# Splitting exponentials between VectorE and GpSimd, three to five, in the first two batches of an attention and mixture-of-experts kernel, with the router sums moved behind the hidden low part

## The reference

```python
attn = jnp.einsum('bhqd,bhkd->bhqk', q, k) * scale
attn = jax.nn.softmax(attn, axis=-1)
out = jnp.einsum('bhqk,bhkd->bhqd', attn, v)
...
g = jnp.einsum('bsh,ehf->ebsf', x, w_gate)
u = jnp.einsum('bsh,ehf->ebsf', x, w_up)
h = jax.nn.silu(g) * u
expert_out = jnp.einsum('ebsf,efh->ebsh', h, w_down)
cw = router_probs * gate_weights
cw = cw / (jnp.sum(cw, axis=-1, keepdims=True) + 1e-09)
out = jnp.einsum('ebsh,bse->bsh', expert_out, cw)
```

## Time and profile before

| | |
|---|---|
| median of three runs | 2798.79 us (2797.85 to 2798.8) |
| profiled execution | 2797.0 us, span 2794.7 us |
| TensorE clock granted, mean | 0.993 |
| busy | PE 2726.0 us (98%), DVE 2173.4 (78%), POOL 1737.4 (62%), ACT 1694.6 (61%) |
| chain that ended last | PE 88%, DVE 6%, ACT 2% |

### The profile page before, as it was taken

How to read it: one execution, slowest core, us unless ns; L and a number is a source line. 1 busy time by engine, 2 the same in 40 slices (tenths; PEclk the granted TensorE clock), 3 DMA queues, 4 the chain that set the end, 5 groups by cost and what they waited for, 6 DMA issues and landing times.

```text
span 2794.7 us, 47289 instructions
## 1 busy us (share of the span) xinstructions
PE 2726.0 (98%) x16416; PEld 2236.9 (80%) x16416; DVE 2173.4 (78%) x3254; ACT 1694.6 (61%) x3240; POOL 1737.4 (62%) x1630
## 2 busy tenths in 40 slices
PE   7789999999999999999999999999999999999998
PEld 5578878888888888878888788888888888888887
DVE  7977788777877787787787888778878778776665
ACT  7756566665666666666665666656666665544443
POOL 5656666666666566666665666765666666655554
PEclk9999999999999999999999999999999999999999
DMA  2113233232323323323232322323223233333332
GB/s 69 39 57 98 77 95 95 89 104 79 95 93 91 103 76 96 95 88 102 80 92 90 99 91 87 95 83 110 90 77 99 76 102 91 95 106 112 107 104 81
DMA packets 251273, 252.25 MB, mean 90 GB/s; under 512 B 15904, under 2 KB 242848, under 8 KB 251040
## 3 DMA queue, kind: packets, MB, share of 16 engines
q1 hardware_dynamic: 251040, 249.25, 29.3%
HBM read 240.66 MB, written 8.52 MB: 89 GB/s over the span
## 4 chain that ended last, share of the span: by engine, by line
PE 88%; DVE 6%; issue 3%; ACT 2%; POOL 0%; DMA 0%; SPq 0%; POOLq 0%; ACTq 0%; DVEq 0%
PE ps_o L692 23%; PE ps_s L658 23%; PE ps_t L658 23%; PE ps_s L751 4%; PE ps_t L761 3%; PE ps_m L547 3%; PE ps_a L733 2%; PE ps_a L735 2%; DVE h_lo L946 1%; PE ps_m L595 1%; PE ps_m L555 1%; PE ps_m L602 1%; DVE hf L941 1%; PE ps_m L610 1%; DVE hf L934 1%
## 5 line engine op out<-in xcount | busy, mean ns | idle before, releaser
L946 DVE TENSOR_TENSOR h_lo<-hf,h_hi 128x512 fp32r<-128x512 f32 x512 | 493.5, 964 | 229.6 <-ACT h_hi L780 221.7
L780 ACT ACTIVATE h_hi<-hf 128x512 fp32r<-128x512 f32 x512 | 323.9, 633 | 466.3 <-DVE hf L941 466.2
L934 DVE SCALAR_TENSOR_TENSOR hf<-hf,ps_s 128x512 f32<-128x512 f32 x512 | 350.4, 684 | 298.7 <-ACT hf L775 293.5
L775 ACT ACTIVATE hf<-ps_s 128x512 f32<-128x512 f32 x512 | 305.5, 597 | 350.8 <-PE ps_s L658 212.7
L1168 POOL TENSOR_TENSOR wg_lo<-stage_w,wg_hi 128x512 fp32r<-128x512 f32 x256 | 339.8, 1327 | 235.5 <-ACT wg_hi L787 235.3
L692 PE MATMUL ps_o<-h_hi,wd_hi 128*128 128x512 f32 x1024 | 401.4, 392 | 18.9 <-DVE h_lo L946 18.9
L1228 POOL TENSOR_TENSOR Pt_lo<-Pt 128x512 f16<-128x512 f32 x256 | 295.0, 1152 | 186.5 <-ACT Pt L913 185.5
L692 PE MATMUL ps_o<-h_lo,wd_hi 128*128 128x512 f32 x1024 | 399.4, 390 | 0.0
L692 PE MATMUL ps_o<-h_hi,wd_lo 128*128 128x512 f32 x1024 | 398.6, 389 | 0.0
L1168 POOL TENSOR_TENSOR wd_lo<-stage_w,wd_hi 128x512 fp32r<-128x512 f32 x256 | 338.1, 1321 | 91.9 <-ACT wd_hi L787 91.9
L941 DVE TENSOR_TENSOR hf<-hf,ps_t 128x512 f32<-128x512 f32 x512 | 351.9, 687 | 38.1 <-PE ps_t L658 0.7
(11 more groups left out here) (190 smaller groups left out, 5135.8 us busy)
## 6 DMA issues: line engine op xcount, KB each, us to landing
stage_w<-in_L_ffn_w_gate_dram SPq DMA_DIRECT2D x256, 256.0 KB, 2.7
stage_w<-in_L_ffn_w_up_dram SPq DMA_DIRECT2D x256, 256.0 KB, 2.9
stage_w<-in_L_ffn_w_down_dram SPq DMA_DIRECT2D x256, 256.0 KB, 2.7
cwb<-d_cw SPq DMA_DIRECT2D x64, 256.0 KB, 3.7
X<-in_x_dram SPq DMA_DIRECT2D x32, 256.0 KB, 3.1
C<-in_fside_BxSxS_dram SPq DMA_DIRECT2D x16, 256.0 KB, 3.0
KVM<-in_ctx_dram SPq DMA_DIRECT2D x16, 256.0 KB, 2.7
d_x<-X SPq DMA_DIRECT2D x16, 256.0 KB, 2.1
```

The costliest lines, as they stand in the source:

```text
L775: act.activation(hf[:], ps_g[:], ACT.Tanh, scale=0.5).then_inc(tanh_done, 1)
L780: act.activation(h_hi[f % FC][:], hf[:], ACT.Copy).then_inc(hh_done, 1)
L934: dve.scalar_tensor_tensor(out=hf[:], in0=hf[:], scalar=1.0, in1=ps_g[:], op0=ALU.add, op1=ALU.mult).then_inc(gate_done, 1)
L946: dve.tensor_tensor(h_lo[f % FC][:], hf[:], h_hi[f % FC][:].bitcast(F32), ALU.subtract).then_inc(hl_done, 1)
```

## The change

Two things change. In batches 0 and 1, which end before the joint stage begins, VectorE takes the items 1, 4 and 6 of each eight (three), and GpSimd the items 0, 2, 3, 5 and 7 (five). From batch 2 on the split is as before. Since the counts per batch now differ, TensorE's waits take their values from a running sum. And in every turn, VectorE's router instructions stand behind h_lo and the weighted outputs of the step instead of ahead of the attention sums.

```diff
@@ -55,6 +55,7 @@
     DVE_LOW = (1, 3, 5, 7)
+    DVE_LOW_ALONE = (1, 4, 6)
@@ -392,12 +393,15 @@
-        def by_dve(i):
-            return i % OCT in DVE_LOW
-
-        def low_parts(i, dve):
-
-            return sum(by_dve(j) == dve for j in range(i))
+        def by_dve(b, i):
+            alone = (b + 1) * STEPS <= START
+            return i % OCT in (DVE_LOW_ALONE if alone else DVE_LOW)
+
+        low_parts = {True: [0], False: [0]}
+        for b in range(B):
+            for i in range(STEPS):
+                for dve in (True, False):
+                    low_parts[dve].append(low_parts[dve][-1] + (by_dve(b, i) == dve))
@@ -719,8 +723,8 @@
                         if i == first:
-                            turn.wait(pe, lo_dve, d, low_parts(i + 4, True))
-                            turn.wait(pe, lo_pool, d, low_parts(i + 4, False))
+                            pe.wait_ge(lo_dve, low_parts[True][(turn.b + d) * STEPS + i + 4])
+                            pe.wait_ge(lo_pool, low_parts[False][(turn.b + d) * STEPS + i + 4])
@@ -1036,8 +1040,6 @@
-                    router_weights(turn, step)
-
                     d, i = item_at(step, 1 - BEHIND)
@@ -1066,12 +1068,13 @@
                         low_of(f + 1)
                     if f is not None and f % EXPERT == EXPERT - 1:
                         weigh_output(f, 1)
+                    router_weights(turn, step)
```

More of the change, by code:

```diff
@@ L225, in bass_xattn_moe_ffn_kernel @@
         t_ps = Count("t_ps", 32); exp_done = Count("exp_done", 32)
-        lo_dve = Count("lo_dve", STEPS // OCT * len(DVE_LOW)); lo_pool = Count("lo_pool", STEPS - lo_dve.per)
+        lo_dve = sem("lo_dve"); lo_pool = sem("lo_pool")
         av_ps = Count("av_ps", 32)
@@ L1068, in body @@
                         weigh_output(f, 1)
+                    router_weights(turn, step)
                     d, i = item_at(step, -1)
-                    if turn.has(d) and by_dve(i):
+                    if turn.has(d) and by_dve(turn.b + d, i):
                         turn.wait(dve, exp_done, d, i + 1)
@@ L1073, in body @@
                         dve.tensor_tensor(Pt_lo[slot][:], Pt[slot][:], Pt[slot][:].bitcast(BF16)[:, 1::2],
-                                          ALU.subtract).then_inc(lo_dve.sem, 1)
+                                          ALU.subtract).then_inc(lo_dve, 1)
                     name, k, d, one, _ = misc(turn, step)
@@ L1224, in body @@
                     d, i = item_at(step, -1)
-                    if turn.has(d) and not by_dve(i):
+                    if turn.has(d) and not by_dve(turn.b + d, i):
                         turn.wait(pool, exp_done, d, i + 1)
@@ L1228, in body @@
                         pool.tensor_tensor(Pt_lo[slot][:], Pt[slot][:], Pt[slot][:].bitcast(BF16)[:, 1::2],
-                                           ALU.subtract).then_inc(lo_pool.sem, 1)
+                                           ALU.subtract).then_inc(lo_pool, 1)
                     for o, at, d in v_at(turn):
```

## The result

The changed kernel takes **2806.7 us** (median of 8 runs, 2804.3 to 2808.16), the kernel before 2798.14 us beside it (8 runs): ratio 1.0031, 95% interval 1.0022 to 1.004. It is slower by 8.6 us; 13 were forecast. The profiled execution took 2804.47 us, its span 2802.5 us against 2794.7, so 7.8 us longer.

The account below looks back on a forecast made before the run. TensorE, busy 98%, bounds the kernel, so only its waits count. Profiled execution 2797.0 + 10 (early stage) + 3 (joint stage) = 2810.0 us; the median lies 1.8 above, 2811.8, said as 2812; range 2796 to 2826.

Parts of the forecast that it names:

- Early stage, +10 forecast: Batches 0 and 1: delayed groups cost 11.7 us, VectorE's relief takes 1.7 off; bounds -5.6 and +19.
- what the last low part loses, each four loses: Early stage: a loop in which TensorE's products with the values wait for the low part of each four's last item.
- relief: Early stage: VectorE's 5.6 us less work shortens TensorE's waits for maxima by a quarter, 1.7 us.
- The fourth row: Early stage, items 47, 51, 55: item 47 has slack for all, 0; items 51 and 55 -0.4 and +0.5 us.
- The split is neutral: Rival, early stage: VectorE's lighter load brings maxima and mq early enough, early 0, joint +3, 2802 us; chance 0.17.
- relief wins: Rival, early stage: half of VectorE's waits go (-3.9 us) and no group is late, 2798 us; chance 0.08.
- Joint stage, +3 forecast: Joint stage: twelve turns each 0.2 us longer, 2.4 us, and 0.3 in each of two turns; bounds -17.6, +15.6.
- The replay of the second step: Joint stage: h_lo done at 357.0 instead of 357.95, TensorE waits 0.4 us; gate product at 360.25 instead of 359.75.
- The gain of 1.0 is given back: Joint stage: TensorE starts 1.0 us earlier after h_lo, then loses that and 0.2 us more per turn.
- The first half of the replay: Joint stage: h_lo, at 349.31, wins against acc's second half, ends at 350.0 instead of 352.17; the 0.92 us wait goes.
- The turn is lost: Rival, joint stage: acc's second half beats h_lo, gate product 1.2 us later, +1.3 us a turn, 2824 us; chance 0.13.
- The router waits really go: Rival, joint stage: moved sums fall into GpSimd's gaps, all 17.6 us of h_lo waits gained, 2791 us; chance 0.12.

Follow-up runs that it names:

- Experiment 3: Kernel before, router unmoved; in batches 0 and 1 VectorE takes items 1, 3, 7 of each eight, GpSimd five: 2796.8 us, ratio 0.9994.
- experiment 4: Kernel before, router unmoved; in batches 0 and 1 VectorE takes items 0, 2, 4, 6 and GpSimd 1, 3, 5, 7: 2813.43 us, ratio 1.0056.
- experiment 2: Kernel before with only the router moved behind h_lo, split 1, 3, 5, 7 kept: 2794.53 us, ratio 0.9992.
- experiment 7: Kernel before, router unmoved, but from batch 2 on item 19's low part goes to GpSimd: 2801.23 us, ratio 1.0013.
- experiment 1: Kernel before with only the split 1, 4, 6 for VectorE in batches 0 and 1, router unmoved: 2806.41 us, ratio 1.0033.
- Experiment 9: Kernel before with the router moved and cprod, css, cden, cw made one-input reciprocals (output numbers differ): 2777.01 us, ratio 0.9928.
- experiment 6: Kernel before with the router moved and, from batch 2 on, item 19's low part on GpSimd; early split unchanged: 2794.79 us, ratio 0.999.

## Why the prediction was right, and where it wasn't

**Early stage, +10 forecast, +8.2 measured.** The step "what the last low part loses, each four loses" held: in 15 of 16 groups TensorE's products start 0.10 to 0.15 us after GpSimd's low part, and experiments 3 and 4 show that it is the item. The two prices held as well: from the exponential's end to the low part's end item 27 takes 0.75 us more than before (forecast 0.8, taken as 0.75) and item 23 1.15 (1.15, taken as 1.2). How much later than before each four's products started, as an increment over the four ahead:

```
items            forecast        measured
3 11 19 27 43 59 6 x 0.75 = 4.5  .92 .76 .66 .53 -.49 1.18 = 3.6
15 23 31 63      4 x 1.2 = 4.8   .52 1.95 1.28 1.29        = 5.0
7 35 39          2.3             .72 1.85 1.04             = 3.6
47 51 55         0.1             -1.54 -.89 .07            = -2.4
behind item 63                   -1.6
relief           -1.7            not separate
sum              10.0            8.2
```

The sizes of the even and odd groups are right within 1 us together; single groups are not. One trace is a weak witness for a single group: in experiment 2, whose code is that of before up to step 51, item 23 is 1.3 us late and items 43 and 47 get 2.5 us back, and in experiment 7 neither happens.

The fourth row failed. The forecast gave item 47 nothing, since it had slack; but its 1.7 us of slack took up delay of the groups ahead, here 1.54 us, and the same 1.54 in experiment 1. This has nothing to do with the router, which comes later. Of items 51, 55 and 59 the router's move took 1.4 us off (experiment 1 has increments of -.57, .72 and 1.60 there), and by the first gate that is gone again. I had priced the move at nothing outside the joint stage; in the change that came out, by luck, since with the splits 1, 3, 5, 7 and 1, 3, 7 the same move gains 3.0 to 3.5 us in the same stretch (experiment 2).

The relief was put at a quarter of the waits for maxima, 1.7 us. No run measures it: in the change it is contained in the increments, and the -1.6 us behind item 63 only look like it (in experiment 1 they are -3.0). So the sum of 8.2 against 10 is in part luck: delays of 12.2 us in the first three rows, against 11.6 forecast, and 4.0 us of recovery, against 1.6, for which the forecast had another reason.

**The split is neutral, relief wins.** Both fell: their 2802 and 2798 us, ratios of 1.0014 and 1.000, lie below the intervals of the change and of experiment 1. (The 3 us in them are the forecast's joint stage, which did not come; without them they lie lower still.) Experiment 3 shows the condition under which they hold, with the last items kept.

**Joint stage, +3 forecast, -0.4 measured.** The replay of the second step came out on the trace (after minus 8.2 us): ATT until 355.2 (forecast 355.1), h_lo done at 356.9 (357.0), cden held until 357.8 (358.0), negmax done at 359.4 (359.6), the gate product at 360.0 (360.25); TensorE's wait for h_lo is 0.38 us (0.4), and the wait for a maximum is new in each of twelve turns. "The gain of 1.0 is given back" is what the three distances show: -0.94, then +0.99. Only the 0.2 us a turn beyond it were too much: it was 0.05 in this turn and 0.2 us in all twelve together, where 2.4 were forecast, and the 0.6 us for two further turns did not come. The first half of the replay was right in its result and wrong on the way: h_lo did not win the race against acc and end at 350.0, but lost it and ended at 351.2 (after minus 8.2 us). TensorE wanted it at 351.3, so the first wait still went, with 0.1 us to spare; that is luck.

**The turn is lost** happened as an event and not as a price. h_lo came at 357.51, as forecast, and acc's second half, at 357.54, went ahead. But the price of 1.3 us a turn was wrong: I let cprod and css each wait for one of GpSimd's instructions. Only cprod waited (0.91); css followed in the same gap (0.15). The gate product then stood at 361.03, where it stood before, shifted. The forecast for the first step, with its win, and this loss meet at the same instruction of GpSimd, the low part ending at 360.29.

**The router waits really go** was refuted for this change and confirmed as a mechanism. It was said to decide from a saving of about 1.0 us of such waiting a turn, and to bring all 17.6 us then. Experiment 9 removes the waiting of the four and brings 17.8 us in the twelve turns. In the change the waiting of css and cw (1.31 and 1.03 us) did go, to 0.15 and 0.17; but cprod, cden, ATT and the first h_lo took it over, with 0.91, 0.99, 1.04 and 1.87 us. Taking each instruction's shortest time off, the router's four, ATT and the two h_lo of the turn shown waited 4.4 us in all before and 4.6 us in the change (an estimate from VectorE's timelines). The rival did not ask who waits in their place.

The rule of the Trainium skill, "SBUF — State Buffer", section "SBUF: two separate sides", that the loser of the port blocks for the whole instruction, agrees with every such line, down to two elements (cden, 0.99 us). The same section of the Trainium skill limits it to VectorE instructions with two SBUF inputs or in a two-port mode; experiment 9 agrees, as its one-input reciprocals took 0.12 to 0.25 us in the same places. The sentence of the Trainium skill, "Perfetto Trace Analysis", section "Optimizing Scalar/DVE Operations", that moving work between the two might not help, is borne out by experiment 6, with nothing gained (joint 2623.8 against 2623.9).

## What to carry to other kernels

Before work is dealt out to two engines, ask which item of each group is waited for, and leave that one on the engine that reaches it first; the count mattered less here (3 to 5 with the right items is free, and 4 to 4 with the wrong ones costs 16 us). Moving short instructions out of the way of a long wait gives back what it gains when they still stand ahead of the next thing that is waited for; measure distances between the starts of one repeated product, step by step, since a list of waits drops the small ones. Where VectorE and GpSimd keep each other waiting, as here, the thing to schedule is the port's time: look for the stretch in which VectorE's short two-input instructions stand, and move GpSimd's work out of it, as the exchange of two items did for 5.8 us.

## What the hardware showed that I had not expected

- Of VectorE's instructions only some wait for GpSimd. In the changed kernel maxima (negmax, 0.63 to 0.69 us in all 512), reciprocals (rsum, 0.19 to 0.20) and the gate product, which has one operand in PSUM (0.67 to 0.69 us in all 512), took the same time whether GpSimd was at work or not. Two of these, negmax and rsum, read PSUM; but the sums lsum and csum, which read SBUF, stayed at 0.12 to 0.18 us as well. Those with two SBUF inputs took up to 1.88 us for 0.68. But so did TENSOR_SCALAR with one tensor in SBUF: 0.40 to 0.41 us in the eight that started beside no instruction of GpSimd, 1.20 us (median, at most 1.39) in the 56 that started inside one.
- The race turns on hundredths. h_lo, dispatched 0.03 us before the start of GpSimd's next half of acc, lost and took 1.87 us; in the twelve turns it was dispatched from 0.04 us before to 0.01 us after that start, and lost every time. In experiment 7 ATT and wu_lo started within 0.01 us of each other, and ATT lost six times of twelve. In the kernel before, an h_lo dispatched well inside an instruction of GpSimd (351.23) went next at its end.
- A TENSOR_TENSOR of two elements held VectorE's queue for 0.99 us, and the waiting of four such small instructions a turn, with what it pushed about, was worth 17 us in 2794 (experiment 9).
